# An offset convolution regrouped: two vertical taps to one 128-row matmul, and a late row of its own

## The reference, cut to what matters

```python
# layer 0: deformable 3x3 convolution on the group-normed input
om = conv3x3(gn(x), w_off) + b_off          # 27 maps: 9 x (dy, dx) offsets and 9 masks
sampled = bilinear(gn(x), grid + om[:18]) * sigmoid(om[18:])   # 4 neighbours, 9 taps
x = x + einsum('bckhw,ock->bohw', sampled, w_conv)
# layer 1: two 3x3 convolutions with ternary weights, batch norm over all batches, relu
h = relu(bn(conv3x3(gn(x), ternary(w1))))
x = x + relu(h + bn(conv3x3(h, ternary(w2))))
```

## Time and profile before

| | |
|---|---|
| median of the runs (lowest, highest) | 2911.25 us (2909.43, 2911.72) |
| profiled execution, its own time | 2900.94 us |
| span of the profile | 2899.2 us |
| mean granted TensorE clock | 0.929 |
| TensorE, VectorE, ScalarE, GpSimd busy | 2443.0, 2264.2, 1274.3, 1440.4 us |

### The profile page before, as it was taken

How to read it: one execution, slowest core, us unless ns; L and a number is a source line. 1 busy time by engine, 2 the same in 40 slices (tenths; PEclk the granted TensorE clock), 3 DMA queues, 4 the chain that set the end, 5 groups by cost and what they waited for, 6 DMA issues and landing times. The chain is left out here.

```text
span 2899.2 us, 38156 instructions
## 1 busy us (share of the span) xinstructions
PE 2443.0 (84%) x12442; PEld 1696.9 (59%) x12442; DVE 2264.2 (78%) x4762; ACT 1274.3 (44%) x2181; POOL 1440.4 (50%) x1270
## 2 busy tenths in 40 slices
PE   4699988869999999899999988998888388999930
PEld 3355555435555666566666655555555388999930
DVE  5788888977888888888888888878886965666665
ACT  3444444445445554555455544444443133322245
POOL 1555555645555565555565556665562803333300
PEclk8799999989999999999999999999898798999965
DMA  8999989988989999999999999998895122111179
GB/s 265 387 348 338 355 334 339 362 295 312 351 336 353 352 354 346 323 346 348 341 354 360 338 349 331 353 342 329 314 337 195 33 86 64 55 52 52 44 288 406
DMA packets 279918, 831.07 MB, mean 287 GB/s; under 512 B 25932, under 2 KB 59724, under 8 KB 279252
## 3 DMA queue, kind: packets, MB, share of 16 engines
q0 software_dynamic: 165888, 604.05, 55.8%
q1 hardware_dynamic: 113876, 225.19, 22.1%
HBM read 743.67 MB, written 85.48 MB: 286 GB/s over the span
## 5 line engine op out<-in xcount | busy, mean ns | idle before, releaser
L503 POOL DMA_INDIRECT G<-pixel_pairs,quad_c x1152 | 1214.7, 1054 | 890.9 <-PE psT L1223 585.8
L995 DVE SCALAR_TENSOR_TENSOR G<-G,wts_c 128x256 f32<-128x256 f32 (+1 forms) x2304 | 1254.7, 612 | 159.2 <-DMA G<-pixel_pairs,quad_c 155.9
L1134 PE MATMUL psD<-ST,wconv 128*128 128x512 f32 x2304 | 1081.3, 614 | 0.0
L602 ACT ACTIVATE G<-G,wts_c 128x256 f32<-128x256 f32 x1152 | 490.2, 497 | 487.9 <-DVE G L995 487.7
L1134 PEld LDWEIGHTS psD<-ST,wconv 128*128 128x128 f32 x2304 | 437.0, 200 | 442.7 <-issue 441.7
L1223 PE MATMUL psT<-idn,G 128*128 128x128 f32 x2304 | 329.9, 290 | 212.1 <-ACT G L602 209.4
L661 ACT ACTIVATE ST<-psT 128x1024 f32<-128x1024 f32 x288 | 293.9, 1020 | 461.1 <-PE psT L1223 460.9
L1223 PEld LDWEIGHTS psT<-idn,G 128*128 128x128 f32 x2304 | 278.7, 149 | 290.8 <-ACT G L602 198.7
L1122 PE MATMUL psF<-pl,qw 128*128 128x256 f32 x1872 | 265.2, 296 | 42.0 <-DVE h1c L852 31.3
L1122 PEld LDWEIGHTS psF<-pl,qw 128*128 128x128 f32 x1872 | 241.3, 192 | 67.0 <-issue 44.8
L1103 PE MATMUL psA<-po,woff 128*64 128x512 f32 x864 | 267.4, 450 | 0.0
(11 more groups left out here) (203 smaller groups left out, 2323.2 us busy)
## 6 DMA issues: line engine op xcount, KB each, us to landing
xx<-in_x SPq DMA_DIRECT2D x56, 512.0 KB, 4.8
pixel_pairs<-yT SPq DMA_DIRECT2D x104, 256.0 KB, 6.1
G<-pixel_pairs,quad_c POOLq DMA_INDIRECT x1152, 6.7
x<-x1c SPq DMA_DIRECT2D x32, 512.0 KB, 5.3
h<-h1c SPq DMA_DIRECT2D x32, 512.0 KB, 10.9
out<-h SPq DMA_DIRECT2D x16, 1024.0 KB, 17.2
xf<-x SPq DMA_DIRECT2D x24, 640.0 KB, 9.3
area<-h SPq DMA_DIRECT2D x24, 640.0 KB, 4.1
```

Source lines behind the costliest of these rows:

```text
L503: pool.indirect_dma_start(out=G[:, i % RING, :], out_offset=None, in_=tbl[d.b].rearrange("y x q c -> (y x) (q c)"), in_offset=bass.Indirec ...
L602: act.activation(g, g, ACT.Copy, scale=wts_c[:, d.p, i:i + 1]).then_inc(d_scaled, 1)
L995: dve.scalar_tensor_tensor(g[:, 0:w], g[:, w:2 * w], wts_c[:, d.p, q * NG + i:q * NG + i + 1], g[:, 0:w], ALU.mult, ALU.add).then_inc(d_ma ...
L1134: ins = pe.matmul(psD[:, oc, :], wconv[:, t, k, oc * 128:(oc + 1) * 128], ST[:, k % 3, t, :], start=(k == 0 and t == 0), stop=(k == TAPS - ...
```

## The change

Nine taps become seven units. The three "pair" units (0, 4, 5; one for each dx) multiply the rows 0 to 7 of the padded chunk by the weights of dy = 0 and dy = 1 side by side, 128 weight columns: accumulator rows 0 to 63 get dy = 0, rows 64 to 127 get dy = 1, which belongs one image row higher. The three "third" units (1, 2, 3) add dy = 2 to rows 0 to 63, as before. The last image row of dy = 1 needs the padded row 8, which the pair units don't read; the "corner" unit (6) makes it with 12 matmuls of 64 pixels and 128 weight columns in a part of another bank (psX at 400 for o, psF bank 1 at 128 for j). The evacuation puts the upper accumulator rows one image row to the left and appends the corner, so that om_c has 128 rows, and the turn sums four groups instead of two with a 128 x 27 `selhl`. The matmuls of a chunk go from 36 of 512 pixels to 24 of 512 and 12 of 64; the evacuation from one ScalarE operation to three. The step at which each unit is issued is in the new tables; the corner waits for all four copies of yT (o) or for the previous `j_sig` (j), and in the last chunk of a z batch TensorE waits for `o_omc` before step 5. The weights are stored by dx first.

```diff
-            woff = sb(one, "woff", [128, CT, TAPS, 64], F32R)
+            woff = sb(one, "woff", [128, CT, 3, 3, 64], F32R)
-            om_c = sb(one, "om_c", [64, PX])
+            om_c = sb(one, "om_c", [128, PX])
-            selhl = sb(one, "selhl", [64, 27])
+            selhl = sb(one, "selhl", [128, 27])
+            ps_corner, ps_jcorner = psX[:, 400:400 + W], psF[:, 1, 128:128 + W]
...
-            J_TAPS = {5: [0, 1], 6: [2, 3], 7: [4, 5], 8: [6, 7, 8]}
-            O_TAPS = {0: [0], 1: [1, 2], 2: [3, 4], 3: [5, 6], 4: [7, 8]}
+            PAIR, THIRD, CORNER = (0, 4, 5), (1, 2, 3), 6
+            OFF_UNITS = range(CORNER + 1)
+            J_UNITS = {5: [0, 1], 6: [2, 3], 7: [4], 8: [5, 6]}
+            O_UNITS = {0: [0], 1: [1], 2: [2, 3], 3: [4], 4: [5, 6]}
...
+                def off_evac(dst, acc, corner):
+                    act.activation(dst[0:64, :], acc[0:64, :], ACT.Identity, bias=boff[:, 0:1], scale=1.0)
+                    act.activation(dst[64:128, 0:PX - W], acc[64:128, W:PX], ACT.Copy)
+                    return act.activation(dst[64:128, PX - W:PX], corner[64:128, :], ACT.Copy)
...
-                    act.activation(om_c[:], psA[0:64, :], ACT.Identity, bias=boff[:, 0:1], scale=1.0).then_inc(o_omc, 1)
+                    off_evac(om_c[:], psA[:], ps_corner).then_inc(o_omc, 1)
...
-                    step(dve.tensor_copy(woff[:, :, :, 0:27], raw_off))
-                    for t in range(CT):
-                        i = dve.tensor_tensor(woff[:, t, :, 32:59], raw_off[:, t], woff[:, t, :, 0:27].bitcast(F32), ALU.subtract)
+                    by_dx = [raw_off[:, t].rearrange("p (y x) j -> p x y j", y=3) for t in range(CT)]
+                    for t in range(CT):
+                        i = dve.tensor_copy(woff[:, t, :, :, 0:27], by_dx[t])
+                    step(i)
+                    for t in range(CT):
+                        i = dve.tensor_tensor(woff[:, t, :, :, 32:59], by_dx[t], woff[:, t, :, :, 0:27].bitcast(F32), ALU.subtract)
...
+                def off_unit(pad, acc, corner, unit):
+                    dx = unit - 3 if unit in (4, 5) else unit - 1 if unit in THIRD else 0
+                    for t in range(CT):
+                        for part in range(2):
+                            begin, end = t == 0 and part == 0, t == CT - 1 and part == 1
+                            if unit in PAIR:
+                                ins = pe.matmul(acc.rearrange("p (h w) -> p h w", h=RC), woff[:, t, dx, 0:2, :].rearrange("p y m -> p (y m)"),
+                                                pad[:, part, t, 0:RC, dx:dx + W], start=(dx == 0 and begin), stop=(dx == 2 and end))
+                            elif unit in THIRD:
+                                ins = pe.matmul(acc[0:64, :].rearrange("p (h w) -> p h w", h=RC), woff[:, t, dx, 2, :],
+                                                pad[:, part, t, 2:2 + RC, dx:dx + W], start=False, stop=False)
+                            else:
+                                for x in range(3):
+                                    ins = pe.matmul(corner, woff[:, t, x, 0:2, :].rearrange("p y m -> p (y m)"),
+                                                    pad[:, part, t, RC, x:x + W], start=(x == 0 and begin), stop=(x == 2 and end))
...
+                    if unit == CORNER:
+                        need(pe, j_sig, 2 * j.n)
+                    ins = off_unit(pj, psF[:, 0, :], ps_jcorner, unit)
...
+                                pe.wait_ge(o_omc, o.n + 1)
                             group_sums((0, z.b))
...
+                                if unit == CORNER:
+                                    need(pe, o_yt, PT * (o.n + 1))
+                                ins = off_unit(po[:, o.p], psA[:], ps_corner, unit)
...
-    sel = np.zeros((64, 27), np.float32)
+    sel = np.zeros((128, 27), np.float32)
+    for first in (0, 32, 64, 96):
+        sel[first + np.arange(27), np.arange(27)] = 1
```

More of the change, by code:

```diff
@@ L187, in build @@
             h1_flat = h1c[:].rearrange("p t x -> p (t x)")
-            jt_om_c = h1_flat[0:64, 0:PX]
+            jt_om_c = h1_flat[:, 0:PX]
             jt_om = h1_flat[:, PX:PX + PT * 27].rearrange("p (t j) -> p t j", t=PT)
@@ L1095, in group_sums @@
                               start=True, stop=True).then_inc(s_gnmm, 1)
-                def conv_tap(c, pad, w, acc, tap, first, last, m):
-                    dy, dx = tap // 3, tap % 3
-                    for oc in range(acc.shape[1]):
-                        for t in range(CT):
-                            for part in range(2):
-                                ins = pe.matmul(acc[:, oc, :].rearrange("p (h w) -> p h w", h=RC), w[:, t, tap, oc * m:(oc + 1) * m],
-                                                pad[:, c.p, part, t, dy:dy + RC, dx:dx + W],
-                                                start=(first and t == 0 and part == 0), stop=(last and t == CT - 1 and part == 1))
+                def off_unit(pad, acc, corner, unit):
[13 more added lines that the diff above has]
+                                                    pad[:, part, t, RC, x:x + W], start=(x == 0 and begin), stop=(x == 2 and end))
                     return ins
@@ L1143, in turn_om, with jt_conv @@
                     ins.then_inc(o_om, 1)
-                def jt_conv(j, tap):
-                    if tap == 0:
+                def jt_conv(j, unit):
+                    if unit == 0:
                         pe.wait_ge(j_split, j.n + 1)
                         need(pe, j_omc, j.n)
-                    dy, dx = tap // 3, tap % 3
-                    for t in range(CT):
-                        for part in range(2):
-                            ins = pe.matmul(psF[0:64, 0, :].rearrange("p (h w) -> p h w", h=RC), woff[:, t, tap, :],
-                                            pj[:, part, t, dy:dy + RC, dx:dx + W],
-                                            start=(tap == 0 and t == 0 and part == 0), stop=(tap == TAPS - 1 and t == CT - 1 and part == 1))
-                    if tap == TAPS - 1:
+                    if unit == CORNER:
+                        need(pe, j_sig, 2 * j.n)
+                    ins = off_unit(pj, psF[:, 0, :], ps_jcorner, unit)
+                    if unit == CORNER:
                         ins.then_inc(j_conv, 1)
@@ L1184, in head @@
                     for r in range(3, 6):
-                        for tap in range(3 * (r - 3), 3 * (r - 2)):
-                            jt_conv(j0, tap)
+                        for unit in OFF_UNITS[3 * (r - 3):3 * (r - 2)]:
+                            jt_conv(j0, unit)
                         turn(r)
@@ L1190, in head @@
                     turn(7)
-                    for tap in range(TAPS):
-                        jt_conv(j1, tap)
+                    for unit in OFF_UNITS:
+                        jt_conv(j1, unit)
                     group_sums((0, 1))
```

16 lines of the change are left out of this document (7 added, 9 removed).

## The result

The changed kernel takes 2883.45 us, the median of 4 runs (2880.65 to 2885.12), against 2910.34 (2907.57 to 2911.72) for the kernel before beside it (the three runs of the section ahead and one more): a ratio of 0.9908 [0.9891, 0.9925], faster by 27 us. In a later series it was 2882.75 (5 runs) against 2906.46, 0.9917 [0.9902, 0.9933], faster by 24. The profiled execution took 2881.93 us, its span is 2880.1, the mean granted clock 0.923 (before 0.929).

The account below looks back on a forecast made before the run. TensorE bounds pass 0 after tap 1; in passes 1 and 2 the VectorE and ScalarE chain leads up to tap 4, then TensorE. -14 + 4 + 1.5 = -8.5 us from 2911.25 gives 2903, range 2885 to 2917.

Parts of the forecast that it names:

- choice of base: Sum made against one profiled execution of 2900.94 us; its difference to the median put on top, 2911.25 - 8.5 = 2902.75.
- the turn over 128 instead of 64 rows: 0: Turn matmuls of the offset convolutions: using 128 rows instead of 64 changes the time by 0.
- here every load uses all rows: TensorE weight loads: all use all rows, so the skill's rule would leave loads unhidden; 2913 us, left 2%.
- passes 1 and 2, 16 chunks: +4: Savings of taps 1 and 3 lie under the VectorE and ScalarE chain, corner adds 0.44; 0.25 a chunk, +4 us.
- the new wait: Last chunks of passes 0 and 1: TensorE waits before tap 5 for the evacuation; covered in pass 0, +1.5 us in pass 1.
- if the longer pauses in passes 1 and 2 bring the lower clock in: Sign of being wrong: longer TensorE waits in passes 1 and 2 bring the lower clock; no size given.
- pass 0: TensorE leads between tap 1 and the last deform matmul, so fewer matmuls shorten the chunks; -14 us.
- the 1.5 us taken off for them: Pass 0: deduction from the 15.3 us saving because gathers will land later; 1.5 us.
- rival B: Nothing comes through: VectorE and gathers also bound pass 0; 2911 us (2906 to 2915), 27%.
- The prices: TensorE cost per matmul: pair and third-row matmuls 236 ns, corner matmuls 115 ns; a convolution 7.04 us instead of 8.50.
- rival C: Slower by the corners: corner matmuls run at the recorded load's pace, 188 ns; +14 us, 2925, 12%.
- Rival A: Every column counts: all saved TensorE time comes through, 30 convolutions x 1.46 = -44 us, 2867; 7%.

Follow-up runs that it names:

- e1_turn128: Kernel before with only om_c, jt_om_c and selhl widened to 128 rows, upper 64 zero; 2902.6 us against 2907.09, ratio 0.998.
- e9_turn_fill: Kernel before with the 128-row turn and eight unread matmuls in step 0 of passes 1 and 2; 2898.91 us against 2907.92, ratio 0.9972.
- e0_before: Kernel before, unedited, profiled a second time; 2909.57 us, span 2907.8.
- e5_before_fill: Kernel before with eight unread matmuls added in step 0 of passes 1 and 2; 2902.31 us against 2907.8, ratio 0.9984.
- e8_after: Changed kernel, unedited, profiled again; span 2889.1 us, pass 1 546.4, pass 2 528.8.
- e3_extra0: Changed kernel with eight unread 512-column matmuls added in step 0 of passes 1 and 2; 2882.23 us against 2906.56 for the kernel before, ratio 0.9918.
- e3_extra4: Changed kernel with the corner unit issued twice in step 4 of passes 1 and 2; 2900.94 us against 2906.56 for the kernel before, ratio 0.9982.

## Why the prediction was right in direction and short in size

**Two steps failed, and one choice of base.** First, "the turn over 128 instead of 64 rows: 0". It is 0.28 us less each time, 30 times inside the passes, 8.4 in the stretches in which it stands; alone, in the kernel before, it brought 3 to 8 us (e1_turn128), and 3.4 with the fill (e9_turn_fill). I had compared the turn's own matmuls and never looked at the weights' rows against those of its neighbours, though the earlier trace rows stand side by side with 64\*128 (64 rows, 128 columns) and 128\*64 in them; "here every load uses all rows" is wrong for the turn, and the 1.00 us of the turn, read as eight times 125 ns, holds 0.19 of the change of rows behind it. Second, "passes 1 and 2, 16 chunks: +4". I let 0.19 of the 1.9 us of taps 1 and 3 come through, which with the corner's 0.44 is +0.25 a chunk. Chunk 12, the sample, measures -0.19 up to tap 4 and +0.37 for the corner; the size was right there and the sample wrong. By the means of the profiles 6.5 us come through in the 16 chunks instead of 3, and the turn takes 4.7 more, so that both passes together, with the new wait, are 1.9 us shorter where 5.5 longer were forecast.

Why more comes through of taps 1 and 3 can be read in chunk 21, in two executions that have the lower clock behind the wait before tap 1. First tap 5 of e0_before (its tap 1 starts at 1527.37, shown with e5_before_fill), then taps 1, 4 and 5 of e8_after:

```profile
1554.85 1.03 PE L1223 MATMUL psT<-idn,G 128*128 128x128 f32 x8
```

```profile
1511.08 1.32 PE L1240 MATMUL psT<-idn,G 128*128 128x128 f32 x8 [2.46 <-ACT G L611]
...
1531.38 1.09 PE L1240 MATMUL psT<-idn,G 128*128 128x128 f32 x8 [1.00 <-ACT G L611]
...
1537.97 1.09 PE L1240 MATMUL psT<-idn,G 128*128 128x128 f32 x8
```

From tap 1 to 5 it is 1554.85 - 1527.37 = 27.48 us before and 26.89 after; the executions without a spell have 25.85 and 25.90. The waits before taps 3 and 4 that the change made are slack, and they take up a part of the spell: from tap 1 to tap 2 it costs 1.6 to 1.7 us in both kernels (8.14 instead of 6.50, 7.22 instead of 5.53), up to tap 5 it is still 1.6 before and only 1.0 after. Chunk 23 is the other case: there the chain doesn't lead at tap 4, and even without a spell it takes 25.4 us from tap 1 to 5 instead of 26.0 (after: e3_extra0, since the profiles of after have the lower clock in it). The prediction's sign of being wrong, "if the longer pauses in passes 1 and 2 bring the lower clock in", came true in part: there are 60 us at the lower clock in the two passes instead of 49. They cost less than the fewer ones did before.

The base: the sum was made against one execution, and its difference to the median put on top. The four profiles of before span 8.6 us, 8.5 of them in pass 2, where the shown one was the fastest, with 17.1 us at the lower clock against up to 30.7. The same step from 2911 down to 2903 was thus no more certain than its own size. By the means of the profiles the forecast -8.5 meets -19.6:

| term | forecast | means of profiles | what differs |
|---|---|---|---|
| pass 0 | -14 | -17.0 | turn -4.3 (e9_turn_fill), so -12.7 for the rest |
| passes 1 and 2, taps 1 to 4 | -3 | -6.5 | more comes through than in chunk 12 |
| taps 4 to 5, corner | +7 | +5.8 | |
| taps 6 to 7, turn | 0 | -4.7 | the turn |
| their other taps | 0 | +1.8 | not followed up |
| new wait in pass 1 | +1.5 | +1.7 | |
| behind, and head | 0 | -0.7 | within executions |

How much of the -6.5 is luck of the three and four executions isn't known, since the spells fall differently in each. The 4 to 7 us between profiled and timed differences stay open.

**Pass 0 was right in its mechanism, and in its number partly by luck.** Chunks 1 to 5 of the shown execution take 62.55, 63.68, 65.09, 66.60 and 63.85 us, mean 64.35 (forecast 64.3). But 0.56 of the 2.7 us that each lost are two turns, which the forecast had at nothing; chunk 0, with 1.4 in the sum, gave nothing (71.45 and 71.50 us by the means), and chunks 6 and 7, with 0, gave 0.9 and 1.9. The wait before tap 1 kept its length, as the timeline of chunk 2 shows beside the earlier trace rows:

```profile
231.22 1.97 PE L1240 MATMUL psT<-idn,G 128*128 128x128 f32 x8 [5.39 <-ACT G L611]
...
```

The waits of TensorE and of VectorE for the same five chunks (161 to 483 us), which answer to the earlier trace rows:

```profile
PE psT L1240 <- ACT G L611: 31.1, 8, 5.4
...
DVE G L1007 <- DMA G<-pixel_pairs,quad_c: 15.9, 22, 1.4
```

Five of TensorE's eight waits are the one before tap 1 (27 us in all, as before); the other three, 1.63, 0.45 and 2.15 us long, lie before taps 4 and 6 of chunk 3 and tap 4 of chunk 4, where TensorE now comes before ScalarE has scaled (in the five chunks before there was one such wait, of 0.2). There the saving meets its end; the forecast had allowed for it in two chunks, with 2.0 instead of 2.8. VectorE does not wait longer for gathers, and the DMA moves 354 GB/s in the pass instead of 344: the 1.5 us taken off for them was not needed, and rival B (nothing comes through) is refuted. Chunk 7 is 1.9 us shorter by the means (75.98 against 77.88), where the new wait was expected to be covered.

**The prices were right.** Pair matmuls lie 0.24 us apart, corner matmuls 112 ns; twelve more corner matmuls made tap 4 to 5 of e3_extra4 1.29 us longer, 108 ns each against the forecast's 115, so rival C (188 ns) is refuted. The recorded loads of the corner are longer than that:

```profile
L1123 PEld LDWEIGHTS psX<-po,woff x288: 187/192/193, 131.0 to 1658.2; 128*128 128x128 f32 x144
```

192 ns of record for a load in a row whose pace is about 110: the records of loads overlap too, and the length of one is no bound of the pace. The evacuation's three operations take 676, 539 and 206 ns (together 0.75 over the old one, forecast 0.8), and no wait behind them grew. The corner's own waits for yT and `j_sig` cost nothing. Tap 4 to 5 took 6.57 us (forecast 6.6), the wait before tap 3 grew by 0.93 (forecast 0.9), that before tap 4 to 0.60 (0.9).

**The new wait** of the last chunks is there. Tap 4 to 5 of chunk 15, after:

```profile
1123.35 1.03 PE L1240 MATMUL psT<-idn,G 128*128 128x128 f32 x8
...
1131.52 0.36 PE L1106 MATMUL psX<-mv,gavg 128*128 128x4 f32 x2 [1.48 <-issue]
1131.73 1.07 PE L1240 MATMUL psT<-idn,G 128*128 128x128 f32 x8
```

8.38 us, before 6.35 (1141.32 to 1147.67): 2.03 more, of which 0.37 is the corner that every chunk has, so 1.7 for the wait where 1.5 were forecast. TensorE stands still for 1.48 of it.

**Rival A** (every column counts, 2867) is refuted by e3_extra0: 31 us of added columns left the time where it was.

## What to carry to other kernels

Cut a period at the places where the engine waits: work removed ahead of such a wait is given back in it while the clock is the same, work removed where there is none comes through nearly whole, and a pair of kernels with work added on each side shows which is which. The wait that grew is not lost altogether: it takes up part of a spell of the lower clock. One chunk is no sample for sixteen; sum each interval over all of them. When an operand changes its number of rows, look at the weight loads of the neighbours too, not at the operation's own time. Before a sum is set on a median, profile the same kernel several times, and take the parts of a period from executions in which the clock agrees.

## What the runs showed of the hardware

- A turn with 64-row weights among 128-row ones costs 0.28 us more than one with 128 rows of which half are zeros: its first load starts 0.94 us after the last of psD's instead of 0.43, and the next unit comes 1.00 instead of 0.81 us after it. Why a change of the row span holds the load back is not shown.
- Waits of TensorE of 2.46 us between the same work were followed by the lower clock in some chunks and not in others. Filling them with matmuls that nobody reads made the kernel before 5.5 us faster and left the time of the changed one as it was (e3_extra0, 0.9918). With the waits of 5.4 us in pass 0 filled as well the changed one is 3 to 6 faster by the medians (0.9897 against 0.9908 and 0.9917, overlapping intervals), and the profiled pass 0 goes from 531.8 to 527.4.
- A spell of the lower clock that made chunk 21 1.6 to 1.7 us longer from tap 1 to tap 2 cost it 1.6 us up to tap 5 in the kernel before, where TensorE doesn't wait in between, and 1.0 in the changed one, where it otherwise waits 0.90 and 0.58 us.
- Twelve matmuls of 64 columns with 128-column weights run at 108 to 112 ns each (108 by the twelve more of e3_extra4), eight transposes of 128 columns at 109.
